# Delta attention on one core: two of four inverse corners multiplied in the other order, alternating with the first two

## What is computed

```python
decay = jnp.exp(jnp.tril(g_diff))
L = -jnp.matmul(kbc, jnp.swapaxes(kc, -1, -2)) * decay
L = jnp.where(tri_incl, 0.0, L)
attn = solve_triangular(eye - L, eye, lower=True)
v_intra = jnp.matmul(attn, vbc)
...
v_new = v_i - jnp.matmul(kcd_i, state)
out_i = jnp.matmul(q_i * jnp.exp(g_i)[..., None], state) + jnp.matmul(a_i, v_new)
new_state = state * jnp.exp(g_last) + jnp.matmul(k_scaled.T, v_new)
```

## Time and profile before

| | |
|---|---|
| median of three runs | 2029.11 us (2028.65 to 2031.85) |
| the profiled execution | 2028.85 us, of which the trace spans 2027.0 |
| granted clock of TensorE, mean over the span | 0.958 |
| PE busy | 1843.1 us (91%) |
| VectorE busy | 1287.5 us (64%) |
| GpSimd busy | 1077.0 us (53%) |
| ScalarE busy | 995.4 us (49%) |

### The profile page before, as it was taken

The page is one execution under the profiler, slowest core; times in us unless marked ns, Lnnn a source line. Parts: engine busy times, 40 slices in busy tenths (PEclk is TensorE's granted clock), DMA queues, the critical chain, the costliest instruction groups (busy, mean ns, idle before and its releaser), DMA issues.

```text
span 2027.0 us, 45825 instructions
## 1 busy us (share of the span) xinstructions
PE 1843.1 (91%) x16855; PEld 1191.5 (59%) x16855; DVE 1287.5 (64%) x2490; ACT 995.4 (49%) x2433; POOL 1077.0 (53%) x2259
## 2 busy tenths in 40 slices
PE   7799997877899896898999999999999999999987
PEld 5422564432243574346777777777777777677775
DVE  2544564695578533627777777777777777777752
ACT  2375232215321452525656656665666566566643
POOL 0521222224100340126887787887878888888873
PEclk7899998998999796999999999999999999999999
DMA  6035422110010632202222222222222222222221
GB/s 157 1 116 156 108 46 53 52 62 1 1 44 7 176 116 88 40 14 56 53 53 64 64 54 54 64 63 55 49 60 54 53 64 64 54 53 64 44 45 32
DMA packets 231181, 124.42 MB, mean 61 GB/s; under 512 B 141360, under 2 KB 210513, under 8 KB 230705
## 3 DMA queue, kind: packets, MB, share of 16 engines
q1 hardware_dynamic: 225008, 111.20, 22.1%
q0 software_dynamic: 5952, 10.29, 2.2%
HBM read 87.94 MB, written 39.74 MB: 63 GB/s over the span
## 4 chain that ended last, share of the span: by engine, by line
PE 23%; POOL 20%; issue 6%; SPq 4%; ACT 3%; DMA 2%; DVE 2%; POOLq 0%; DVEq 0%; ACTq 0%
POOL a_term L2591 8%; POOL a_z L2595 8%; PE ps L2043 5%; PE ps L2053 3%; PE ps L2242 3%; SPq L1976 2%; POOL a_rstd L2567 2%; POOL a_xnorm L2573 2%; PE ps L2273 2%; DMA a_l<-a_v_dram 1%; SPq L1984 1%; PE ps L2229 1%; PE ps L2160 1%; PE ps L2209 1%; PE ps L2283 1%
## 5 line engine op out<-in xcount | busy, mean ns | idle before, releaser
L2591 POOL TENSOR_TENSOR a_term<-a_z,a_l 32x14 f32<-32x14 f32 (+6 forms) x896 | 342.8, 383 | 70.3
L2595 POOL TENSOR_TENSOR a_z<-a_z,a_term 32x14 f32<-32x14 f32 (+6 forms) x896 | 339.6, 379 | 70.2
L2621 DVE SCALAR_TENSOR_TENSOR a_qkv<-a_raw,a_taps,a_qkv 128x1024 f32<-128x1024 f32 x192 | 247.1, 1287 | 6.1
L2043 PE MATMUL ps<-all_xn,a_w_qkv 128*128 128x512 f32 x512 | 246.7, 607 | 0.0
L390 POOL DMA_INDIRECT f_rows<-a_row,a_slots x32 | 35.4, 1105 | 184.6 <-DVE a_of_tile L380 139.2
L2242 PE MATMUL ps<-a_out_t,a_w_out 128*128 128x256 f32 x512 | 130.7, 399 | 1.9 <-ACT a_out_t L2465 1.7
L2043 PEld LDWEIGHTS ps<-all_xn,a_w_qkv 128*128 128x128 f32 x512 | 89.2, 193 | 69.1 <-issue 67.3
L2386 ACT ACTIVATE a_raw<-ps 128x512 f32<-128x512 f32 x128 | 76.4, 598 | 108.2 <-PE ps L2043 107.5
L2053 PE MATMUL ps<-a_w_z,all_xn 128*128 128x256 f32 x512 | 122.6, 383 | 0.0
L2585 POOL COPY a_z<-a_l 32x256 f32<-32x256 f32 x64 | 27.1, 423 | 154.6 <-DMA a_l<-a_v_dram 154.4
L850 POOL DMA_INDIRECT f_sums<-a_y,a_xs x23 | 36.1, 1568 | 136.3 <-ACT a_y L799 133.4
(11 more groups left out here) (331 smaller groups left out, 4304.7 us busy)
## 6 DMA issues: line engine op xcount, KB each, us to landing
a_gc_rows<-a_g_dram SPq DMA_DIRECT2D x64, 256.0 KB, 4.8
a_v_dram<-a_v SPq DMA_DIRECT2D x64, 256.0 KB
a_w<-in_f_w SPq DMA_DIRECT2D x24, 512.0 KB, 4.5
a_w_qkv<-in_a_w SPq DMA_DIRECT2D x16, 512.0 KB, 3.9
a_t_dram<-a_z SPq DMA_DIRECT2D x512, 8.0 KB
a_w_z<-in_a_w SPq DMA_DIRECT2D x16, 256.0 KB, 2.9
a_w_out<-in_a_wo SPq DMA_DIRECT2D x16, 256.0 KB, 3.1
a_v_off<-a_v SPq DMA_DIRECT2D x256, 4.0 KB
```

What stands on the lines that cost most here:

```text
L2043: mm = pe.matmul(ps[:, to, :], w_qkv[:, k, mt * P:(mt + 1) * P], xn[:, k, b * T:(b + 1) * T], start=k == 0, stop=k == KC - 1)
L2591: pool.tensor_tensor(term[:, 0:j, j + 1:], z[:, 0:j, j:j + 1].broadcast_to([HP, j, n]), rows[:, j:j + 1, j + 1:].broadcast_to([HP, j, n]), ...
L2595: pool.tensor_tensor(z[:, 0:j, j + 1:], z[:, 0:j, j + 1:], term[:, 0:j, j + 1:], ALU.add).then_inc(sub_step, 1)
L2621: dve.scalar_tensor_tensor(to, rows, tap, to, ALU.mult, ALU.add).then_inc(conv_ready if j == TAPS - 1 else conv_step, 1)
```

## The change

Of the four matrices of a window, the first two (NEAR = 2) are joined as before. The last two (FAR = 2) take their product in the other order, from the other half: first v0 from the SECOND half with the lower block of `inv`, then that result with the FIRST half. For this their `v0` is needed untransposed, as `v_far`, made from `k k^T` and a decay of its own, `decay_far`; and their `t_half` copy gets the factor beta. In `join_c` and `close_c` a matmul of the first kind and one of the second kind alternate, which lie in different quarters of the 128x128 array.

```diff
                 def join_c(w):
                     pe.wait_ge(th_ready, w + 1)
-                    for r in range(PR):
-                        mm = pe.matmul(upper(BW)[SECOND, r, :], v0[FIRST, w % 3, r, SECOND], t_half[FIRST, r, :], ...)
+                    pe.wait_ge(zh_ready, w + 1)
+                    pe.wait_ge(far_ready, w + 1)
+                    for r in range(NEAR):
+                        pe.matmul(upper(BW)[SECOND, r, :], v0[FIRST, w % 3, r, SECOND], t_half[FIRST, r, :], ...)
+                        mm = pe.matmul(upper(BW)[FIRST, r, :], v_far[SECOND, w % 3, r, :],
+                                       inv[SECOND, w % 2, NEAR + r, SECOND], ...)
...
                 def close_c(w):
                     pe.wait_ge(wc_ready, w + 1)
-                    pe.wait_ge(zh_ready, w + 1)
-                    for r in range(PR):
-                        mm = pe.matmul(bank(BZ)[FIRST, r, SECOND], wc[SECOND, r, :], z_half[SECOND, r, :], ...)
+                    pe.wait_ge(t_far_ready, FAR * (w + 1))
+                    for r in range(NEAR):
+                        pe.matmul(bank(BZ)[FIRST, r, SECOND], wc[SECOND, r, :], inv[SECOND, w % 2, r, SECOND], ...)
+                        mm = pe.matmul(upper(BH)[FIRST, r, :], t_half[FIRST, NEAR + r, :], wc[FIRST, r, :], ...)
...
+                def make_decay_far(w):
+                    act.wait_ge(gc_loaded[w % 2], 16 * (w // 2 + 1))
+                    if w >= 1:
+                        act.wait_ge(far_ready, w)
+                    for r in range(FAR):
+                        act.activation(decay_far[SECOND, r, :], gc_rows[SECOND, w % 2, NEAR + r, FIRST], ACT.Exp,
+                                       bias=gate(K_GC, w, NEAR + r)[SECOND, :], scale=-1.0).then_inc(decay_far_ready, 1)
...
+                def copy_top(w):
+                    act.activation(inv[FIRST, w % 2, :, FIRST], bank(BZ)[FIRST, :, FIRST], ACT.Copy)
+                def copy_far(w):
+                    for r in range(NEAR, PR):
+                        act.activation(t_half[FIRST, r, :], lower(BH)[FIRST, r, :], ACT.Copy,
+                                       scale=gate(K_NBETA, w, r)[FIRST, :]).then_inc(t_far_ready, 1)
...
-                    act.activation(wc[SECOND, :, :], upper(BW)[SECOND, :, :], ACT.Copy).then_inc(wc_ready, 1)
+                    act.activation(wc[:, :, :], upper(BW)[:, 0:NEAR, :], ACT.Copy).then_inc(wc_ready, 1)
-                def copy_whole(w):
+                def copy_corners(w):
                     act.wait_ge(c_psum, w + 1)
-                    act.activation(inv[:, w % 2, :, :], bank(BZ), ACT.Copy).then_inc(inv_ready, 1)
+                    act.activation(inv[FIRST, w % 2, 0:NEAR, SECOND], bank(BZ)[FIRST, 0:NEAR, SECOND], ACT.Copy)
+                    act.activation(inv[FIRST, w % 2, NEAR:, SECOND], upper(BH)[FIRST, 0:FAR, :],
+                                   ACT.Copy).then_inc(inv_ready, 1)
...
+                def make_far(w):
+                    dve.wait_ge(kq_ready, w + 1)
+                    dve.wait_ge(decay_far_ready, FAR * (w + 1))
+                    dve.tensor_tensor(v_far[SECOND, w % 3, :, :],
+                                      bank(BK)[SECOND, 3, FIRST].unsqueeze(1).broadcast_to([P // 2, FAR, P // 2]),
+                                      decay_far[SECOND, :, :], ALU.mult).then_inc(far_ready, 1)
...
-                    dve.tensor_copy(z_half[SECOND, :, :], bank(BZ)[SECOND, :, SECOND]).then_inc(zh_ready, 1)
+                    dve.tensor_copy(inv[SECOND, w % 2, :, SECOND], bank(BZ)[SECOND, :, SECOND]).then_inc(zh_ready, 1)
```

More of the change, by code:

```diff
@@ L1797, in delta_and_looked_up @@
     FIRST, SECOND = slice(0, P // 2), slice(P // 2, P)
+    NEAR, FAR = VPK, PR - VPK
     PITCH = SB * PR * P + SB
@@ L1852, in delta_and_looked_up @@
         wa, wb, za, tb = (s.buf(n, [P, PR, HP]) for n in ("wa", "wb", "za", "tb"))
-        wc, z_half, t_half = (s.buf(n, [P, PR, P // 2]) for n in ("wc", "z_half", "t_half"))
+        t_half = s.buf("t_half", [P, PR, P // 2])
+        wc = s.buf("wc", [P, NEAR, P // 2])
+        decay_far, v_far = s.buf("decay_far", [P, FAR, P // 2]), s.buf("v_far", [P, 3, FAR, P // 2])
         inv = s.buf("inv", [P, 2, PR, P])
@@ L2124, in close_a @@
                         pe.wait_ge(th_ready, w)
+                        pe.wait_ge(t_far_ready, FAR * w)
                     for r in range(PR):
@@ L2158, in join_c @@
                     pe.wait_ge(th_ready, w + 1)
-                    for r in range(PR):
-                        mm = pe.matmul(upper(BW)[SECOND, r, :], v0[FIRST, w % 3, r, SECOND], t_half[FIRST, r, :],
-                                       start=True, stop=True)
+                    pe.wait_ge(zh_ready, w + 1)
+                    pe.wait_ge(far_ready, w + 1)
+                    for r in range(NEAR):
+                        pe.matmul(upper(BW)[SECOND, r, :], v0[FIRST, w % 3, r, SECOND], t_half[FIRST, r, :],
+                                  start=True, stop=True)
+                        mm = pe.matmul(upper(BW)[FIRST, r, :], v_far[SECOND, w % 3, r, :],
+                                       inv[SECOND, w % 2, NEAR + r, SECOND], start=True, stop=True)
                     mm.then_inc(wc_psum, 1)
@@ L2166, in close_c @@
                     pe.wait_ge(wc_ready, w + 1)
-                    pe.wait_ge(zh_ready, w + 1)
-                    for r in range(PR):
-                        mm = pe.matmul(bank(BZ)[FIRST, r, SECOND], wc[SECOND, r, :], z_half[SECOND, r, :],
+                    pe.wait_ge(t_far_ready, FAR * (w + 1))
+                    for r in range(NEAR):
+                        pe.matmul(bank(BZ)[FIRST, r, SECOND], wc[SECOND, r, :],
+                                  inv[SECOND, w % 2, r, SECOND], start=True, stop=True)
+                        mm = pe.matmul(upper(BH)[FIRST, r, :], t_half[FIRST, NEAR + r, :], wc[FIRST, r, :],
                                        start=True, stop=True)
@@ L2495, in _ @@
                 act.wait_ge(gates_ready, 1)
+                make_decay_far(0)
                 make_decay(0)
@@ L2506, in _ @@
                 f_silu(3)
+                make_decay_far(1)
                 make_decay(1)
@@ L2521, in _ @@
                     if made(w + 2):
+                        make_decay_far(w + 2)
                         make_decay(w + 2)
@@ L2545, in _ @@
                         copy_wc(w)
+                        copy_top(w)
+                        copy_far(w)
                     if silus:
@@ L2551, in _ @@
                     if made(w):
-                        copy_whole(w)
+                        copy_corners(w)
                     part(w, 3)
@@ L2747, in _ @@
                 dve.memset(v0_off[:, :, :, :], 0.0).then_inc(filled_raw, 1)
-                dve.wait_ge(filled_raw, 2)
+                dve.memset(inv[:, :, :, :], 0.0).then_inc(filled_raw, 1)
+                dve.wait_ge(filled_raw, 3)
                 dve.wait_ge(small, SMALL * 16)
@@ L2788, in _ @@
                 make_v0(0)
+                make_far(0)
                 f_mul(1)
@@ L2800, in _ @@
                 make_v0(1)
+                make_far(1)
                 f_mul(4)
@@ L2825, in _ @@
                     if made(w + 2):
+                        make_far(w + 2)
                         make_at(w + 2)
```

6 lines of the change are left out of this document (5 added, 1 removed).

## The result

The changed kernel took **2057.4 us** (median of five runs, 2046.31 to 2060.93), the kernel before beside it 2029.11 (2018.87 to 2031.85): 1.0127 times as long, 95% interval 1.0099 to 1.0156. A second series, on another occasion, gave 2050.22 us (2046.86 to 2055.0) and 1.009 (1.0071 to 1.0109). So it is slower by 0.9 to 1.3%, where 2032 us, within 2018 to 2044, had been forecast.

What follows compares the result with a forecast made beforehand. Rounds were taken as bound by three full POOL turns plus one path over the other engines; 2028.85 + 0 + 4.9 - 2 = 2031.75 us profiled, median 0.26 above: 2032 us, range 2018 to 2044.

Steps and rivals of the forecast that it cites:

- What bounds the kernel: Delta-attention loop: a round of four turns, 69.25 us, is three full POOL turns plus one 19.19 us path over other engines.
- Part 1: join_c and close_c on PE: pairs in two quarters overlap, 0.23 us less a call, 29 us less PE work.
- The rival that the pairs do not overlap: join_c and close_c: calls stay long in both, 2041 us; for the join alone 2036; together 8%.
- Part 2: ACT, turns 1 into 2 modulo 4: added small operations spend PE's 0.46 us gain, 0 us on the path.
- the faster rival: ACT's small operations overlap more, so PE's 0.46 us comes through to v0 in turns 1 to 2 modulo 4: 2021 us, 28%.
- the one of ACT's queue: ACT's eight small operations cost 0.3 us each with no overlap, passing into decay, v0 and POOL: 2041 us, 22%.
- Part 3: join_c, turns 2 modulo 4: PE waits 1.70 us for DVE's copy in 14 turns; add_out and v0 0.53 later.
- Part 4: POOL: about 0.2 us of slack after v0, so 0.35 us lost a round, +4.9 us, between 0 and +11.
- The forecast's last sentence: Forecast wrong if POOL were not full, or if join_c's wait shifted the whole round: 14 x 1.24 = +17 us.
- Part 5: Ends: last six turns gain at most 2.8 us, taken as -2; the head's new memset costs 0, bound 1 us.

Runs made afterwards that it cites:

- the copy's place corrected: Changed kernel with DVE's copy of the second half ahead of convolution steps 1 and 2 in late turns too: 2027.52 us, 0.9981 of the kernel before.
- experiment on the order: Changed kernel with both near matmuls ahead of both far ones in join_c and close_c: 2052.7 us, 1.0111 of the kernel before.
- filled kernel: Changed kernel with seven full matmuls, their result unread, on PE ahead of join_c's waits in late turns: 2042.12 us, 1.0046 of the kernel before.
- wait alone: Kernel before with one line more, join_c also waiting for zh_ready (DVE's copy of the second half): 2054.03 us, 1.0108 of the kernel before.

## Why the prediction was wrong, step by step

**What bounds the kernel: right in the main.** A round is three nearly full POOL turns and one path over the other engines, and PE's spare time buys next to nothing: the copy's place corrected, 29 us less PE work gave 0.9981 against 0.9992. But POOL was less full than the two turns that were read: of its 22 waits before, 10 fell into the other three turns, 7 us in all. (POOL's instructions in this trace name no PSUM tile; they work on SBUF.)

**Part 1, the pairs: right.** A call took 605 ns from its first start to the next instruction in the kernel before and 378 to 385 in all that have the pairs: 0.23 us, as worked out. Join_c's two row tiles share bank BW and started 0.01 us apart (above), so the rule that the Trainium skill states in TensorEngine Tiling (Array Packing), Restrictions and Gotchas, that they cannot be in one bank at a time, did not hold for this case, in which the output partitions differ. The rival that the pairs do not overlap is out. The Trainium skill, in TensorE: Matmul & The Clock Gate, The mechanism, has matmuls start and end in program order, without reordering; for passes of different quarters the recorded starts of the experiment on the order show otherwise (1581.29 for the first far pass, 1581.44 and 1581.50 for near ones that stand ahead of it in the program).

**Part 2, ACT: right in the sum, by luck.** From POOL's start in turn 33 to the end of v0 it was typically (median of twelve) 12.96 us before and 12.93 after, where 0 had been forecast: all of PE's 0.46 us was spent on ACT. This timeline of ACT, after, answers to the earlier trace rows:

```profile
1516.50 0.26 ACT L2473 ACTIVATE a_wc<-ps 128x128 f32<-128x128 f32 x1
1516.66 0.37 ACT L2464 ACTIVATE a_inv<-ps 64x256 f32<-64x256 f32 x1
1516.92 0.50 ACT L2468 ACTIVATE a_t_half<-ps,a_gates 64x64 f32<-64x64 f32 x2
...
1520.17 0.27 ACT L2477 ACTIVATE a_inv<-ps 64x128 f32<-64x128 f32 x1 [0.17 <-PE ps L2183]
...
1522.11 1.28 ACT L2427 ACT_TABLE_LOAD   x1
1523.41 0.58 ACT L2427 ACTIVATE a_decay_far<-a_gc_rows,a_gates 64x64 f32<-64x64 f32 x2
1524.01 0.63 ACT L2432 ACTIVATE a_decay<-a_low 128x512 f32<-128x512 f32 x1
```

The two of `decay_far` held ACT for 0.60 us (1523.41 to 1524.01), not 0.40; the copies were a little cheaper than priced, and ACT still waited 0.17 us for PE where none had been forecast. The errors cancel. Neither the faster rival nor the one of ACT's queue happened. That `decay_far` alone costs 0.3 to 0.6 us a round on the path, the three kernels with it moved show together (3.1 to 7.4 us in twelve rounds).

**Part 3, the wait: its size right, its effect too small.** 1.70 us had been worked out; 1.76 was the mean over the late turns, and `add_out` waited nearly as forecast (0.46 + 0.53 = 0.99 us by the forecast, 1.08 with the clock up). But v0 of the next turn came 0.82 us later in the filled kernel (from v0 to v0 17.33 us against 16.51), not 0.53. In that turn DVE waits for the decay as well, 0.13 us on average in the filled kernel and 0.34 in the row of 1543.81, and not at all in the two kernels with the wait but without `decay_far`. The rest of the 0.29 us was not traced.

**Part 4, POOL: the first step that failed.** I had taken 0.2 us of slack between v0 and POOL, from two turns whose distances were 6.23 and 6.4 us, and so 0.35 us a round, 0.8 at most. In the filled kernel none of that slack shows: from the end of v0 to POOL's start it was 6.65 us on average over the rounds before and 6.77 there, and POOL waited in all twelve rounds instead of three. With longer waits some slack was used (6.35 us in the changed kernel, 6.27 with the wait alone). Over the rounds this distance scatters from 5.9 to 7.7 us, far more than the 0.2 that I read out of two turns. The price with the clock up is **0.92 us a round instead of 0.35**, above its own bound; 14 rounds are 13 us instead of 4.9. The forecast's last sentence, "if the PE wait of 1.7 us shifted the whole round", named this as what would make it wrong, at 1.24 a round. Three quarters of that came with the pairs; without them it was 1.66 of a wait of 1.78.

**What no step contained: the clock.** The earlier trace rows has the clock at 1.00 in the steady rounds, and I priced the wait as idle time only. Behind 8 or 9 of these twelve waits the clock fell to 0.50 for 3.4 us, and `project_out` took 2.7 to 3.6 instead of 1.99 us. In the two executions of the changed kernel a round with a fall lasted 71.8 us and one without 70.4: 1.4 us each (0.9 in the first, 1.9 in the second), 13 us for nine falls by this count, 10.2 by the filled kernel. By the filled kernel the two failures are 11.1 and 10.2 of the 21.3 us.

**Part 5, the ends.** At the end the pairs' gain had been taken as 2 us. From turn 54 to the end it was 165.1 us with the copy's place corrected and 165.9 before, so 0.8 in single executions, which differ by as much on their own. The head held no cost of the memset that can be seen: what was lost before turn 6 is not lost with the copy's place corrected (POOL's first start of the stretch stands at 1025.4 there, 1024.49 before).

## What to carry to other kernels

A wait added to the busiest engine is priced by following what is queued behind it to the engine that sets the round, and slack is granted there only if it was measured over many rounds. Work saved on one engine is worth next to nothing while the queue of another ends at the same time: here moving two small operations behind the one that is waited for gave more (0.9981 to 0.9943) than the pairs themselves (0.9992 to 0.9981). Whoever adds a wait to a nearly full TensorE reads the granted clock behind it, and where a wait is for a copy, the copy can often be put earlier on its own engine.

## What the runs showed of the hardware

- A wait of about 1.8 us in a TensorE that was 97% busy before let the granted clock fall from 1.00 to 0.50 for 3.4 us, but not each time: in twelve rounds behind 8 or 9 waits of the changed kernel, one in the execution with the other order in the calls, three without the pairs. Which waits it hits differs from execution to execution, and the time goes with it: the kernel with `decay_far` moved took from 2033.71 us at a mean clock of 0.957 to 2060.4 at 0.943.
- Matmuls that do nothing can pay for themselves: seven in each such wait brought 2057.4 and 2050.22 down to 2042.12 us. They gained nothing that could be told where the clock had fallen three times in twelve rounds (2054.03 and 2053.7 us).
- Passes of fp32 matmuls in two different quarters of the array ran side by side whatever their order in the program: eight passes of 64x64 in 0.38 us, against 0.605 in one quarter, two row tiles writing one bank on different partitions included.
- Two operations of 64x64 on ACT, with Exp and a bias from SBUF, held it 0.60 us; two copies of 64x128 from PSUM 0.33 (1520.17 to 1520.50 in the timeline).
